# Softmax denominators in attention: more blocks summed outside TensorE, joined by an accumulating DMA

## The reference

```python
q = (x @ wq_w + wq_b).reshape(bs, sl, Q_H, HEAD_DIM)
k = (x @ wk_w + wk_b).reshape(bs, sl, KV_H, HEAD_DIM)
v = (x @ wv_w + wv_b).reshape(bs, sl, KV_H, HEAD_DIM)
qg = q.reshape(bs, sl, KV_H, FACTOR, HEAD_DIM)
attn = jnp.einsum('bqhfd,bkhd->bhfqk', qg, k) * scale
att = jax.nn.softmax(attn, axis=-1)
a = jnp.einsum('bhfqk,bkhd->bqhfd', att, v)
return a.reshape(bs, sl, DIM) @ wo_w + wo_b
```

## Time and profile before

| what | value |
|---|---|
| median of three runs | 2967.85 us |
| profiled execution | 2971.44 us |
| its span | 2969.6 us |
| TensorE matmuls busy | 2880.7 us, 97% |
| VectorE busy | 1931.5 us, 65% |
| GpSimd busy | 1798.1 us, 61% |
| ScalarE busy | 1526.4 us, 51% |
| first and last exp (L879) of attention | 660.4 and 2439.7 us |

### The profile page before, as it was taken

The page is one execution under the profiler, slowest core; times in us unless marked ns, Lnnn a source line. Parts: engine busy times, 40 slices in busy tenths (PEclk is TensorE's granted clock), DMA queues, the critical chain, the costliest instruction groups (busy, mean ns, idle before and its releaser), DMA issues. The chain is left out here.

```text
span 2969.6 us, 49916 instructions
## 1 busy us (share of the span) xinstructions
PE 2880.7 (97%) x15654; PEld 1735.6 (58%) x15654; DVE 1931.5 (65%) x2575; ACT 1526.4 (51%) x2906; POOL 1798.1 (61%) x595
## 2 busy tenths in 40 slices
PE   6999999979999999999999999999999988999998
PEld 4788888854444444444444444444444436888886
DVE  4433333247777777777777777777777736766666
ACT  3211111126666666666666666666666652444444
POOL 2433333237888888888888888888888875211110
PEclk9999999979999999999999999999999998999998
DMA  7543434341211221211221221221221105333331
GB/s 252 177 144 133 160 116 162 100 147 33 53 46 46 52 46 46 52 48 44 52 51 41 52 53 39 52 55 37 52 56 36 42 14 165 107 107 106 106 106 64
DMA packets 158501, 241.46 MB, mean 81 GB/s; under 512 B 48992, under 2 KB 90400, under 8 KB 158368
## 3 DMA queue, kind: packets, MB, share of 16 engines
q1 hardware_dynamic: 158368, 240.05, 27.9%
HBM read 159.12 MB, written 79.82 MB: 80 GB/s over the span
## 5 line engine op out<-in xcount | busy, mean ns | idle before, releaser
L899 DVE TENSOR_REDUCE mx<-s_ps 128x1 f32<-128x1024 f32 x1024 | 1203.9, 1217 | 430.4 <-PE s_ps L968 422.8
L879 ACT ACTIVATE p_t<-st_ps 128x512 f32<-128x512 f32 x2048 | 1113.4, 595 | 553.2 <-PE st_ps L994 484.2
L837 POOL TENSOR_TENSOR p_sum<-p_sum,p_t 128x2048 f32<-128x2048 f32 x256 | 1173.2, 4583 | 22.1
L994 PE MATMUL st_ps<-q_st,k_st 98*128 98x512 f32 x2048 | 809.6, 435 | 11.0 <-ACT p_t L879 7.9
L994 PEld LDWEIGHTS st_ps<-q_st,k_st 98*128 98x128 f32 x2048 | 344.8, 187 | 604.2 <-ACT p_t L879 414.2
L968 PE MATMUL s_ps<-k_st,q_st 96*128 96x512 f32 x2048 | 657.6, 403 | 14.7 <-DMA q_st<-q_hi_d 11.0
L1008 PE MATMUL num_ps<-p_t,v_sb 128*32 128x512 f32 x4096 | 546.4, 605 | 0.9 <-ACT p_t L879 0.9
L837 POOL TENSOR_TENSOR p_sum<-p_t 128x2048 f32<-128x2048 f32 x64 | 293.3, 4583 | 295.0 <-ACT p_t L879 295.0
L968 PEld LDWEIGHTS s_ps<-k_st,q_st 96*128 96x128 f32 x2048 | 389.6, 191 | 95.4 <-DVE mx L899 14.0
L413 POOL TENSOR_TENSOR o_lo<-side,o_hi 128x512 fp32r<-128x512 f32 x80 | 103.9, 1300 | 313.6 <-ACT o_hi L383 313.5
L1279 POOL TENSOR_TENSOR a_lo<-a_f,a_hi 128x1024 fp32r<-128x1024 f32 x32 | 76.1, 2377 | 359.2 <-ACT a_hi L1314 359.1
(11 more groups left out here) (129 smaller groups left out, 2809.4 us busy)
## 6 DMA issues: line engine op xcount, KB each, us to landing
q_st<-q_hi_d SPq DMA_DIRECT2D x128, 256.0 KB, 4.4
stage<-w_mod SPq DMA_DIRECT2D x48, 512.0 KB, 6.6
q_hi_d<-o_hi SPq DMA_DIRECT2D x64, 256.0 KB, 2.0
q_lo_d<-o_lo SPq DMA_DIRECT2D x64, 256.0 KB, 2.0
q_st<-q_lo_d SPq DMA_DIRECT2D x64, 256.0 KB, 4.1
att_d<-a_sb SPq DMA_DIRECT2D x128, 128.0 KB, 2.3
a_f<-att_d SPq DMA_DIRECT2D x32, 512.0 KB, 4.6
x_sb<-x SPq DMA_DIRECT2D x32, 512.0 KB, 5.3
```

The source lines that it names most:

```text
L837: nc.gpsimd.tensor_tensor(total, before, p_t[:, kt, :, :], ALU.add).then_inc(sum_done, 1)
L879: nc.scalar.activation(p_t[:, s, c, :], st_ps[:, c % 2, :], ACT.Exp, scale=SCALE)\
L899: nc.vector.tensor_reduce(mx[:, slot % 2, e:e + 1], s_ps[:, e % 2, :], AX_X, ALU.max)\
L994: nc.tensor.matmul(st_ps[:, c % 2, :], k_st[:, slot // 2, s * P:(s + 1) * P], q_st[:, slot, jj, h * QW:(h + 1) * QW], start=True, stop=True)\
```

## The change

GpSimd adds six blocks as before, but 0, 1, 2, 5, 6 and 7, still with five adds. Blocks 3 and 4 are added by VectorE, a quarter at a time, with a reduction over two elements (`add_two`, into the new tile `two_sum`): quarters 0 to 2 in steps 5 to 7, quarter 3 in step 0 of the next pair. Then GpSimd issues a DMA (`join`) that adds `two_sum` to `p_sum` in SBUF. TensorE sums this one operand over the keys, in step 7 of the next pair. For the last pair alone there is no join; two operands are summed. The division moves by a pair: VectorE does its transpose, reciprocal and transpose in steps 1 to 3 two pairs later, and writes the second transpose to the new SBUF tile `rden`; GpSimd does the product, after its second add. `num_sb` becomes two deep. SyncE's store moves ahead of `put_max` and stands two pairs behind.

VectorE, one pair of the loop before, from the last maximum of step 3 on: `mx` are maxima, `den_t`, `rden_c` and `a_sb` the division, `m_lo` the split maxima; register instructions stand between.

The diff, cut to its core (`total`, `pair` and `slot` as in the functions above):

```diff
-    SUMMED = 6
-    SUMS = SUMMED - 1
-    RAWS = NKT - SUMMED
-    SUM_STEP = 3
+    ADDED = (0, 1, 2, 5, 6, 7)
+    SUMS = len(ADDED) - 1
+    TWO = 3
+    TWO_STEPS = (5, 6, 7)
+    SUM_STEP = 7
+    DIVIDE_STEPS = (1, 2, 3)
+    DIVIDE_AFTER = 2
...
+                    if not below(pair, 2):
+                        store(pair - 2, slot % 2)
                     if not is_int(pair, NPAIR - 1):
                         put_max(pair + 1, (slot + 1) % QR)
-                    if not below(pair, 1):
-                        store(pair - 1, (slot - 1) % 2)
...
+                def join(pair, par):
+                    pool.wait_ge(sum_done, pair * SUMS + SUMS)
+                    pool.wait_ge(two_done, pair * REP + REP)
+                    pool.sem_inc(waited_pool, 1)
+                    nc.gpsimd.dma_start(p_sum[:, par, :, :].rearrange("p c q -> p (c q)"),
+                                        two_sum[:, :, :].rearrange("p c q -> p (c q)"), accum_op=ALU.add)\
+                      .then_inc(joined, 16)
...
+                def divide(pair, par):
+                    pool.wait_ge(rden_step, pair * 2 + 2)
+                    pool.wait_ge(num_taken, pair + 1)
+                    if not below(pair, 2):
+                        pool.wait_ge(a_out[par], (pair - par) * (8 * NQW))
+                    nc.gpsimd.tensor_tensor(a_sb[:, par, :], rden[:, :], num_sb[:, par, :], ALU.mult).then_inc(a_ready, 1)
...
-                            if s < SUMMED:
-                                act.wait_ge(sum_done, (pair - 1) * SUMS + max(s, 1))
+                            if s in ADDED:
+                                act.wait_ge(sum_done, (pair - 1) * SUMS + max(ADDED.index(s), 1))
                             else:
-                                act.wait_ge(den_done, (pair - 1) * RAWS + (s - SUMMED + 1))
+                                act.wait_ge(two_done, (pair - 1) * REP + REP)
...
+                def add_two(pair, c):
+                    dve.wait_ge(exp_done, pair * TILES + ((TWO + 1) * REP + c + 1))
+                    if c == 0 and not below(pair, 1):
+                        dve.wait_ge(joined, pair * 16)
+                    nc.vector.tensor_reduce(two_sum[:, c, :], p_t[:, TWO:TWO + 2, c, :].rearrange("p s q -> p q s"),
+                                            AX_X, ALU.add).then_inc(two_done, 1)
...
-                        if s > SUM_STEP and not below(pair, 1):
-                            divide(pair - 1, (slot - 1) % 2, s - SUM_STEP - 1)
+                        if s == 0 and not below(pair, 1):
+                            add_two(pair - 1, REP - 1)
+                        if s in TWO_STEPS:
+                            add_two(pair, TWO_STEPS.index(s))
+                        if s in DIVIDE_STEPS and not below(pair, 2):
+                            divide(pair - 2, DIVIDE_STEPS.index(s))
...
-                        if s < RAWS and not below(pair, 1):
-                            add_den(pair - 1, SUMMED + s)
                         if s == SUM_STEP and not below(pair, 1):
                             add_sum(pair - 1, (slot - 1) % 2)
```

More of the change, by code:

```diff
@@ L823, in _ @@
                                             wo_hi[:, k, :].bitcast(F32), ALU.subtract).then_inc(wo_lo_done, 1)
+                def join(pair, par):
[5 more added lines that the diff above has]
+                      .then_inc(joined, 16)
                 def do(pair, slot, it):
+                    if not below(pair, 1):
+                        join(pair - 1, (slot - 1) % 2)
                     total = p_sum[:, slot % 2, :, :]
-                    for kt in range(1, SUMMED):
+                    for n, kt in enumerate(ADDED[1:]):
                         pool.wait_ge(exp_done, pair * TILES + (kt * REP + REP))
-                        if kt == 1:
+                        if n == 0:
                             if not below(pair, 2):
                                 pool.wait_ge(sum_used, pair - 1)
-                            before = p_t[:, 0, :, :]
+                            before = p_t[:, ADDED[0], :, :]
                         else:
-                            pool.wait_ge(sum_done, pair * SUMS + (kt - 1))
+                            pool.wait_ge(sum_done, pair * SUMS + n)
                             before = total
                         nc.gpsimd.tensor_tensor(total, before, p_t[:, kt, :, :], ALU.add).then_inc(sum_done, 1)
+                        if kt == DIVIDE_AFTER and not below(pair, 2):
+                            divide(pair - 2, slot % 2)
+                def divide(pair, par):
[4 more added lines that the diff above has]
+                    nc.gpsimd.tensor_tensor(a_sb[:, par, :], rden[:, :], num_sb[:, par, :], ALU.mult).then_inc(a_ready, 1)
                 pairs(pool, do)
+                divide(NPAIR - 2, NPAIR % 2)
+                divide(NPAIR - 1, (NPAIR - 1) % 2)
             @block.scalar
@@ L951, in _ @@
                 pairs(dve, do)
-                for piece in range(4):
-                    divide(NPAIR - 1, (NPAIR - 1) % 2, piece)
+                add_two(NPAIR - 1, REP - 1)
+                for pair in (NPAIR - 2, NPAIR - 1):
+                    for piece in range(3):
+                        divide(pair, piece)
             @block.tensor
@@ L980, in turn_max @@
                         pe.wait_ge(m_lo_done, 1)
-                    elif not is_int(pair, 0):
-                        pe.wait_ge(den_taken, pair - 1)
+                    elif not below(pair, 3):
+                        pe.wait_ge(den_taken, pair - 2)
                     nc.tensor.matmul(m_ps, mx[:, slot % 2, :], ident[:, :], start=True, stop=True)\
@@ L1010, in add_num, with add_sum, add_two @@
                     last.then_inc(num_done, 1)
[L1012 to L1016, removed]
+                def add_sum(pair, par):
+                    last = is_int(pair, NPAIR - 1)
+                    if last:
+                        pe.wait_ge(sum_done, pair * SUMS + SUMS)
+                        pe.wait_ge(den_taken, NPAIR - 1)
+                    else:
+                        pe.wait_ge(joined, pair * 16 + 16)
+                        if is_int(pair, NPAIR - 2):
+                            pe.wait_ge(den_taken, NPAIR - 2)
                         else:
-                            pe.wait_ge(a_ready, pair)
+                            pe.wait_ge(m_lo_done, pair + 3)
                     for c in range(REP):
[L1020 to L1026, removed]
+                        done = nc.tensor.matmul(den_ps[c * HD:(c + 1) * HD, :], ones[:, :], p_sum[:, par, c, :],
+                                                start=True, stop=not last)
+                    done.then_inc(sum_used, 1)
+                def add_two(pair):
+                    pe.wait_ge(two_done, pair * REP + REP)
                     for c in range(REP):
-                        last = nc.tensor.matmul(den_ps[c * HD:(c + 1) * HD, :], ones[:, :], p_sum[:, par, c, :],
+                        done = nc.tensor.matmul(den_ps[c * HD:(c + 1) * HD, :], ones[:, :], two_sum[:, c, :],
                                                 start=False, stop=True)
-                    last.then_inc(sum_used, 1)
+                    done.then_inc(two_used, 1)
                 def entries(pair, part):
@@ L1079, in _ @@
                 add_num(NPAIR - 1, QR - 1, STEPS - 1)
-                for s in range(SUMMED, NKT):
-                    add_den(NPAIR - 1, s)
                 add_sum(NPAIR - 1, (NPAIR - 1) % 2)
+                add_two(NPAIR - 1)
 def finish(nc, x, b_o, lora_in, lora_out, earlier_in, ident, wo_hi, wo_lo, att_d, mod_raw_d, mod_gate_d, out):
```

43 lines of the change are left out of this document (22 added, 21 removed).

## The result

The changed kernel takes 2884.69 us (median of 4 runs, 2883.82 to 2886.12) where the kernel before took 2967.72 (2967.16 to 2969.75) on the same chip: ratio 0.972, 95% interval 0.9703 to 0.9736. That is 83 us faster. The forecast was 2932: its sign was right, the gain more than twice the 36 that it gave, and the time lies in its range. The profiled execution took 2886.12, its span is 2884.3 (before: 2969.6).

What follows compares the result with a forecast made beforehand. TensorE was taken as the bound: 27.61 us a pair falls to 25.89, plus 1.17 of stalls for VectorE, 27.06. A gain of 0.55 on 61 pairs, with branch and ends, nets -36 us: 2932, range 2860 to 3000.

Steps and rivals of the forecast that it cites:

- The TensorE term: Attention pairs: two of three denominator blocks go, 2 x 0.86 = 1.72 us a pair, TensorE period 25.89.
- The reduction: VectorE's four added two-block reductions a pair, ahead of the maxima of steps 5, 6, 7 and 0: 1.15 us each.
- the slow strided rival: VectorE's two-block reductions cost 2.28 us each, stalls 5.69 a pair, time about 3210; chance 0.10.
- VectorE's stall sum: TensorE stalls on VectorE's backlog: 0.10, 0.66, 0.10, 0.31 in steps 5, 6, 7, 0; 1.17 us a pair.
- The three smaller stalls: TensorE's forecast waits for VectorE in steps 5, 7 and 0: 0.10, 0.10 and 0.31 us.
- fixed limit of 1.05: VectorE backlog in us above which TensorE stalls: gap 0.85 plus 0.15 to 0.31, taken as 1.05.
- The term `m_lo`: VectorE's work on m_lo in step 6, counted as 0.37 us of backlog.
- the rival "no stall": VectorE's backlog never passes 1.05, so the whole 1.72 us is gained on 63 pairs: 2865; chance 0.12.
- signs that the prediction gave for being wrong: Steps 6 to 0 run at 3.1, GpSimd has no idle time, or the DMA releases VectorE's step 5 reduction.
- The branch: Behind the loop's branch, 15 times, an extra 0.44 us absorbs step 0's 0.31 stall: 4.7 us in all.
- The rival "GpSimd becomes the bound": DMA issue uses up GpSimd's spare 1.5 us; at a 4.6 issue, period 29.17 and time 3065; chance 0.13.
- The rival of the late join: Joining DMA lands past 11.6 us, VectorE waits before step 5's maxima; at 13.0, 0.7 a pair, 2975; chance 0.10.

Runs made afterwards that it cites:

- b_noden: Kernel before the change, with the two denominator blocks of steps 0 and 1 (blocks 6 and 7) left out; 2876.51 us, ratio 0.9693.
- n_neither: Changed kernel with most of step 7's denominator block cut, no joining DMA and two-block reductions on 16 of 512 columns; 2837.54 us, ratio 0.9559.
- n_both: Changed kernel with step 7's denominator block cut to 32 columns of one quarter in all pairs but first and last; 2874.24 us, ratio 0.968.
- a_step0: Changed kernel with its denominator block moved from step 7 to step 0 of the pair after, everything computed; 2879.08 us, ratio 0.9704.
- n_smallv: Changed kernel with most of step 7's denominator block cut, join kept, two-block reductions on 16 of 512 columns; 2865.0 us, ratio 0.9655.
- n_nojoin: Changed kernel with most of step 7's denominator block cut and the joining DMA replaced by a semaphore increment; 2871.86 us, ratio 0.967.
- b_u8: Kernel before the change, with eight pairs in a loop round instead of four; 2998.85 us, ratio 1.0106.

## Why the prediction was right, and where it failed

**The TensorE term** was right: 1.72 forecast for two blocks, 1.62 and 1.63 found (b_noden, and 27.64 to 26.01 itself). It lacks some 0.09, in step 0, which takes 3.19 in b_noden and n_neither too; I put that down to ScalarE's copy of the numerator, which stands among the step's exps (0.59 us), and no run takes the copy out.

**The reduction** was taken at 1.15 and is issued every 1.17 (1524.67 to 1525.83); the slow strided rival is out. The 16-byte line of the Trainium skill ("SBUF — State Buffer", "Specifications (TRN2)") would have this order of reading run below full bandwidth; the trace has 1243 ns for it beside 1209 for a maximum that reads in a row, so the measurement decides against it here.

**The step that failed is VectorE's stall sum: "step 6: 1.05 - 0.86 + 0.37 + 1.15 = 1.71, stall 0.66", and with it the 1.17 a pair.** The backlog was there: the maxima of step 6 were 0.67 late. The reader was right too: TensorE needs them at the third load of step 7's group, where I expected the stall. But the change itself had put the 0.86 block in front of that load. I used this block to lower step 7's backlog and forgot that it also moves the deadline of step 6's maxima. n_both shows the stalls the moment the block goes (0.2 to 0.3 each in steps 7, 0 and 1), a_step0 shows the 0.2 of step 7. The three smaller stalls failed by the same fixed limit of 1.05 in every step. Steps 5 and 7 have 0.2 and 0.86 more free time than the others, so their maxima start only 0.14 and 0.13 late. In step 0 the maxima are 0.44 late (1535.23 + 0.67 = 1535.90 against 1536.34), and its 3.19 is the same as in b_noden, which has no two-block reductions: the 0.31 is nothing. So in a step without a block the room before TensorE stops is at least 0.44, where the sum had 0.20. The term `m_lo` was also too dear: 0.19 on VectorE (1528.10 to 1528.29), not 0.37. That the time lies inside the range is no merit of this sum: what happened is the rival "no stall" (2865, chance 0.12), for a reason that it didn't give, the block as a cover. It was 20 us too low for 0.09 on each of 49 pairs, some 0.9 on each of 13 pairs with the branch, and 3.6 at the end.

An ordinary pair gained 1.63, not 0.55: over 49 pairs the difference is 53 us, and the whole miss is 47. Two of the signs that the prediction gave for being wrong came true: steps 6 to 0 run at 3.1 but for the block, and GpSimd has no idle time in an ordinary pair.

**The branch** was worth a gain of 0.81 a pair where I summed 0.55 + 0.31 = 0.86: nearly the right number for a wrong reason. Nothing stalled there to be absorbed; instead one of the two blocks removed had been in a wait already (b_noden). There are 13 such pairs between the marks, not 15.

**GpSimd**: 25.6 forecast, 25.96 to 25.99 found. The issue at 0.88 was near the 1.0 assumed, but the wait for the addition ahead of it (0.67) and the slower addition behind it (0.3) were missing. The promised idle time of 1.5 is not there in an ordinary pair. The rival "GpSimd becomes the bound" missed by some 0.04 us a pair: it is what n_smallv shows once the reductions and the block are gone.

**The join** lands after 7.0 (forecast 7.7, and an estimate of 4.4 by the Trainium skill's formula in "DMA: Bandwidth & Descriptors", "Anatomy of one DMA — SWDGE (gpsimd) path", with which this trace does not agree). It is issued 7.15 into the pair (1540.82 - 1533.67), VectorE's first reduction comes at 17.0 (1524.67 + 26.00 - 1533.67): 2.9 to spare. The rival of the late join was right about the place and had less room than 11.6 - 7.7 said. Its 13.0 for a doubled moving part should have been 13.8 on the prediction's own slope (1.5 fixed and twice 6.1), and its 2975 some 2999.

**The end** cost 7.6 where I had 4.0: the wait of 7.13 and the low clock behind it, which nearly doubled both sums (1.94 and 1.93 for 1.04). The last two pairs gain 1.6 each (forecast 1.72). **Pair 0**, forecast at +1.5: between it and the first loop pairs, steps 7, 0 and 1 without a block take 3.26, 3.44 and 3.43, some 0.8 together.

## What to carry to other kernels

A late result costs nothing until its reader comes: put each stall at the instruction that reads, list what the change puts between the two, and give every step its own limit. A block of work that an engine gives up may have been the cover of another engine's lateness, and beside a loop's branch a block of work may cost nothing because its engine would wait there anyway. Take an operation out by itself to see what lies under it, before adding up its time. When three engines come within 0.15 us of the same period, as here, the next gain is in the ends and in the place of what is left, which were worth 13 us.

## What the runs showed of the hardware

- A reduction of 1024 elements read in two rows 8 KB apart took 1243 ns, one that reads them from the score banks 1209.
- An accumulating DMA of 1 MB from SBUF to SBUF landed 7.0 us after its issue and disturbed nothing that the steps show (n_both against n_nojoin). On GpSimd its issue took 0.88, with the next addition starting after 0.61; a wait of 0.67 stood ahead of it, and the addition behind it took 4.89 for 4.59 without the DMA (n_nojoin).
- A loop round of twice the length made a pair with a branch take 33.9 us on the mean where it took 28.2 (b_u8), with 2.02 MB of instruction fetches for 0.64. The shorter round fetched nothing over that queue between 900 and 1700 us, the longer one 46 packets.
- After a wait of 7.13 us TensorE's granted clock was 0.50, and a sum of eight matmuls (512 columns each) took 1.94 for 1.04 at 1.00.
